# A two-layer token kernel on one Trainium2 core: token sums in PSUM columns, six chunks scaled by ScalarE, new engine orders in the paired part

## What is computed

```python
q     = relu(cond @ W3 + b3)                      # (64, 512), one row per batch
v_sum = sum(x, axis=1, keepdims=True)             # over the 64 tokens of a batch
x1    = (64 * x + v_sum) * q[:, None, :]          # the scaled input
y     = relu(x1 @ W2 + b2)                        # 4096 tokens, 512 x 512
out   = x + y @ W_base + b_base + (y @ A_s) @ B_s + sum_e gate_e * (y @ A_r[e]) @ B_r[e]
```

## Time and profile before

| what | us |
|---|---|
| median of 3 runs (240.29 to 241.37) | 240.49 |
| the profiled execution | 240.08 |
| its span, first to last instruction | 238.3 |
| TensorE busy | 227.8 (96%) |
| VectorE busy | 181.5 (76%) |
| GpSimd busy | 120.5 (51%) |
| ScalarE busy | 94.3 (40%) |
| mean granted TensorE clock | 0.986 |

### The profile page before, as it was taken

How to read it: one execution, slowest core, us unless ns; L and a number is a source line. 1 busy time by engine, 2 the same in 40 slices (tenths; PEclk the granted TensorE clock), 3 DMA queues, 4 the chain that set the end, 5 groups by cost and what they waited for, 6 DMA issues and landing times.

```text
span 238.3 us, 2849 instructions
## 1 busy us (share of the span) xinstructions
PE 227.8 (96%) x982; PEld 183.8 (77%) x982; DVE 181.5 (76%) x321; ACT 94.3 (40%) x181; POOL 120.5 (51%) x107
## 2 busy tenths in 40 slices
PE   7999999999999999999949999999899899999994
PEld 3877888888888888888836888888587678888883
DVE  0695799899799996999945699999995578482344
ACT  2369612736244512754135068243313465530010
POOL 4189323365219778699789203369988920000000
PEclk9999999999999999999995999999999999999999
DMA  6999905322294791044179135002155234002044
GB/s 204 323 226 228 255 13 130 70 89 91 35 216 179 231 263 25 1 174 178 26 170 194 44 133 178 0 0 33 21 191 176 88 105 164 0 7 47 11 179 176
DMA packets 32917, 29.05 MB, mean 122 GB/s; under 512 B 5841, under 2 KB 23317, under 8 KB 32902
## 3 DMA queue, kind: packets, MB, share of 16 engines
q1 hardware_dynamic: 31090, 28.69, 42.7%
q10 hardware_dynamic: 1812, 0.17, 0.6%
HBM read 18.89 MB, written 8.39 MB: 114 GB/s over the span
## 4 chain that ended last, share of the span: by engine, by line
PE 66%; POOL 15%; DVE 11%; ACT 3%; issue 2%; DVEq 0%; POOLq 0%; ACTq 0%
PE m_ps L1207 50%; PE hT L1207 7%; PE m_ps L1239 5%; POOL x_lo L483 4%; POOL xs L406 4%; DVE xs L942 3%; POOL x_lo_more L483 3%; DVE xs L928 2%; DVE x_nat L908 2%; POOL xs L496 2%; PE m_ps L1184 2%; POOL xs L502 2%; DVE vsum_pair L935 1%; POOL xs L489 1%; ACT y_hi L565 1%
## 5 line engine op out<-in xcount | busy, mean ns | idle before, releaser
L406 POOL TENSOR_TENSOR xs<-xs,qT 128x512 f32<-128x512 f32 x28 | 30.9, 1102 | 50.1 <-DVE xs L782 31.4
L1207 PE MATMUL m_ps<-Wb_lo,y_hi 128*128 128x512 f32 x116 | 45.1, 389 | 0.0
L1207 PE MATMUL m_ps<-Wb_hi,y_hi 128*128 128x512 f32 x116 | 45.1, 389 | 0.0
L1207 PE MATMUL m_ps<-Wb_hi,y_lo 128*128 128x512 f32 x116 | 45.1, 389 | 0.0
L565 ACT ACTIVATE y_hi<-m_ps,condT 128x512 fp32r<-128x512 f32 x30 | 20.8, 692 | 24.5 <-PE m_ps L1207 15.5
L1207 PEld LDWEIGHTS m_ps<-Wb_hi,y_lo 128*128 128x128 f32 x116 | 21.8, 188 | 4.6
L1207 PEld LDWEIGHTS m_ps<-Wb_lo,y_hi 128*128 128x128 f32 x116 | 21.8, 188 | 4.5
L1207 PEld LDWEIGHTS m_ps<-Wb_hi,y_hi 128*128 128x128 f32 x116 | 21.8, 188 | 4.5
L908 DVE TENSOR_TENSOR x_nat<-m_ps,x_nat 128x512 f32<-128x512 f32 x29 | 18.9, 682 | 7.3 <-PE m_ps L1207 7.3
L797 DVE TENSOR_TENSOR y_lo<-m_ps,y_hi 128x512 fp32r<-128x512 f32 x30 | 20.1, 675 | 5.4 <-ACT m_ps L566 5.4
L1207 PE MATMUL m_ps<-x_hi,W_hi 128*128 128x512 f32 x61 | 23.7, 389 | 0.0
(11 more groups left out here) (179 smaller groups left out, 486.0 us busy)
## 6 DMA issues: line engine op xcount, KB each, us to landing
out_dram<-x_nat SPq DMA_DIRECT2D x32, 256.0 KB, 2.1
x_quart<-in_x_dram SPq DMA_DIRECT2D x28, 256.0 KB, 5.0
x_nat<-in_x_dram SPq DMA_DIRECT2D x7, 1024.0 KB, 5.1
gatesT<-wT SPq DMA_DIRECT2D x24, 48.0 KB
x_nat<-in_x_dram SPq DMA_DIRECT2D x4, 256.0 KB, 3.8
W_f<-in_L_cond_W_dram SPq DMA_DIRECT2D x4, 256.0 KB, 6.6
Wb_f<-in_L_ffn_W_base_dram SPq DMA_DIRECT2D x1, 1024.0 KB, 9.3
W_sb<-in_L_cond_W_dram SPq DMA_DIRECT2D x2, 256.0 KB, 4.8
```

Source lines behind the costliest of these rows:

```text
L406: return nc.gpsimd.tensor_tensor(per_batch(tile), per_batch(tile), qT[:, c, BG * g:BG * (g + 1)].unsqueeze(2).to_broadcast([P, BG, N]), AL ...
L1207: mm = nc.tensor.matmul(psum, lhsT, rhs, start=start and i == 0, stop=stop and i == len(terms) - 1)
```

## The change

Names are those of the changed file; p is the pair, i the place in `CHUNKS`.

1. **Sums in PSUM.** `sums_of(p, i)` puts the eight token sums of a chunk in spare columns of a PSUM bank: all eight chunks in pair 0, chunks 1, 2 and 3 in pair 1 (the others stay in `vsum_pair`). The same for the last two chunks of group 3 (`sums_of_x`). TensorE waits before it writes such a bank until the sums are read (`wait_sums_read`, and a wait on `x1_sum_ready`).
2. **Six chunks scaled by ScalarE.** For the three chunks of each pair in `BY_SCALAR` VectorE no longer writes 64 x + sum over 128x512, but only `offset` = sum x q, 128x8; ScalarE then makes (64 q) x + offset in place, batch by batch, eight instructions of 128x64 (`make_chunk`). GpSimd does not touch these chunks. `q64` = 64 q is made once by ScalarE near the start.
3. **Orders.** VectorE handles chunk 3 of pair 0 before `y_rest_single(3, 0)`, and all chunks but chunk 7 ahead of `rank_experts(3)`; in the pairs `rank_experts`/`gates` go ahead of the sums of a chunk, `weigh(g)` behind chunk 4's transpose, `C11(0)` ahead of `weigh(3)`, and `total_next(0)` as a whole ahead of `add_x(3, 0, 1)`. ScalarE and GpSimd follow. TensorE's products keep their order; pair 1's first products wait for fewer `add_x`.

```diff
+        q64 = sb("q64", [P, KC, BG * (NG - PAIRED)])
+        offset = sb("offset", [P, 6, BG])
+        BY_SCALAR = (((0, 0), (1, 2), (0, 1)), ((0, 0), (0, 1), (1, 1)))
...
+        def sums_of(p, i):
+            cols = slice(400 + BG * i, 400 + BG * (i + 1))
+            if p == 0:
+                return m1_ps[1 if i in (4, 5) else 2][:, cols]
+            if i in (1, 2, 3):
+                return m1_pair[0][1][3][:, cols]
+            return vsum_pair[i % 2][:, :]
...
+            def make_chunk(p, half, c):
+                n = nth_by_scalar(p, half, c)
+                act.wait_ge(offset_ready, n)
+                for b in range(BG):
+                    toks = slice(b * N, (b + 1) * N)
+                    which = BG * (2 * p + half) + b
+                    nc.scalar.activation(xs[half][:, c, toks], xs[half][:, c, toks], ACT.Identity,
+                                         bias=offset[:, n - 1, b:b + 1],
+                                         scale=q64[:, c, which:which + 1]).then_inc(act_full_ready, 1)
...
             x1_split(3, 3)
+            make_chunk(0, 0, 0)
             operand(0, "x11", 0)
+            make_chunk(0, 1, 2)
+            operand(0, "T1", 0)
             relu(3, 0)
-            operand(0, "T1", 0)
...
                 operand_next("T4", 0)
                 operand_next("x11", 1)
+                if more:
+                    make_chunk(p + 1, 1, 1)
                 operand_next("x21", 1)
+                if more:
+                    hw_split(g + 1)
                 operand_next("T1", 1)
...
             def add_pair(p, i):
+                if by_scalar(p, i):
+                    g = PAIRED + 2 * p + half
+                    nc.vector.tensor_tensor(offset[:, nth_by_scalar(p, half, c) - 1, :], sums_of(p, i),
+                                            qT[:, c, BG * g:BG * (g + 1)], ALU.mult).then_inc(offset_ready, 1)
...
                 if p == 0:
+                    C11(0)
                     weigh(g - 1)
-                    C11(0)
                     u_2(0)
                     hw_rest(g - 1)
                     turn_next(0)
                     y_rest_pair(0, 0)
-                    sum_next(0)
+                    total_next(0)
                     add_x(g - 1, 0, 1)
...
                 if p > 0:
-                    pe.wait_ge(out_ready, TT * (g - 2) + TT)
+                    pe.wait_ge(out_ready, TT * (g - 2) + 2)
                 blocks(0, 1)
+                if p > 0:
+                    pe.wait_ge(out_ready, TT * (g - 2) + 3)
+                else:
+                    wait_sums_read(pe, 0, 4, 5)
                 blocks(0, 2)
```

More of the change, by code:

```diff
@@ L645, in operand @@
                 else:
-                    act.wait_ge(pair_full_ready, nth_chunk(p, {"x11": 0, "x21": 0, "x22": 1}[name], kk + (0 if name == "x11" else 2)))
+                    wait_full(act, p, {"x11": 0, "x21": 0, "x22": 1}[name], kk + (0 if name == "x11" else 2))
                 if p > 0:
@@ L690, in _ @@
             operand(0, "x22", 0)
+            operand(0, "T2", 0)
             relu(3, 2)
-            operand(0, "T2", 0)
             operand(0, "T3", 0)
+            operand(0, "x21", 0)
+            make_chunk(0, 0, 1)
             relu(3, 3)
-            operand(0, "x21", 0)
-            head(3)
             operand(0, "T4", 0)
             operand(0, "x11", 1)
+            head(3)
+            operand(0, "x21", 1)
             exponentials(3)
-            operand(0, "x21", 1)
             operand(0, "T1", 1)
@@ L1152, in pair @@
                 turn_next(2)
+                rank_experts(g)
+                gates(g)
                 total_next(2)
-                rank_experts(g)
                 turn_next(3)
-                gates(g)
                 total_next(3)
                 rank_experts(g + 1)
+                gates(g + 1)
                 turn_next(4)
-                gates(g + 1)
-                total_next(4)
+                weigh(g)
+                sum_next(4)
+                hw_rest(g)
+                add_next(4)
                 turn_next(5)
-                weigh(g)
-                sum_next(5)
-                hw_rest(g)
-                add_next(5)
+                total_next(5)
                 turn_next(6)
                 total_next(6)
-                add_x(g, 0, 1, 2, 3)
+                add_x(g, 0, 1)
                 turn_next(7)
+                total_next(7)
                 weigh(g + 1)
-                total_next(7)
-                hw_rest(g + 1)
+                if more:
+                    hw_rest(g + 1)
+                    add_x(g, 2, 3)
+                else:
+                    add_x(g, 2, 3)
+                    hw_rest(g + 1)
             for p in range(PAIRS):
@@ L1217, in m1 @@
                     pe.wait_ge(wT_ready, g)
+                    if g == PAIRED - 1:
+                        wait_sums_read(pe, 0, 0, 1, 2, 3)
+                elif m == 0 and g == PAIRED - 1:
+                    pe.wait_ge(x1_sum_ready, KC * (g + 1))
                 for k in range(KC):
@@ L1445, in pair @@
                 pe.wait_ge(wT_ready, g + 2)
+                if not last:
+                    wait_sums_read(pe, p + 1, 1, 2, 3)
                 m2(g + 1, 1, *range(KC))
```

116 lines of the change are left out of this document (79 added, 37 removed).

## The result

| | before | after |
|---|---|---|
| median of the runs | 240.44 (4 runs) | 233.83 (4 runs, 233.62 to 234.24) |
| ratio | | 0.972, 95% interval 0.969 to 0.975 |
| the profiled execution / its span | 240.08 / 238.3 | 233.62 / 231.9 |
| mean granted clock | 0.986 | 1.0 |
| TensorE busy | 227.8 | 225.0 (97%) |

A second measurement of the changed kernel, beside the kernel before at 241.22, gave 233.81 (ratio 0.970, 0.968 to 0.972). The prediction was 234.0, with a range of 230.6 to 236.6.

What follows compares the result with a forecast made beforehand. TensorE, busy 227.8 of 238.3, bounds the kernel; only 10.2 of idle or slowed time could be won. 240.08 - 5.2 (pair 0) - 1.3 (pair 1) = 233.6, with the median 0.4 above: 234.0, range 230.6 to 236.6.

Steps and rivals of the forecast that it cites:

- Sums in PSUM: VectorE's token sums with the addend in PSUM: 0.68 each against a mean of 1.13, saving VectorE 0.45 each.
- Pair 0, size: Pair 0 on TensorE: of 6.6 lost, 0.4 stays for T2's rest and 1.0 for u4, gain 5.2.
- The slow stretch: Pair 0, 127 to 131: ten matmuls at granted clock 0.50 after TensorE stood still 3.08; none expected behind 122.
- Pair 0, cause: Pair 0: its waits end with chunk 7, ready on VectorE at 120.6, then GpSimd's scale, T2 and rest.
- The step by step count: Pair 0 through VectorE, ScalarE and GpSimd: chunk 7 at 116.4 instead of 120.6, T2 at 119.2, its rest at 122.5.
- Pair 1, size: Pair 1 on TensorE: of 3.6 lost, 1.3 gained, with bounds 3.6 to -0.4.
- the sign named: Pair 1 on TensorE's timeline: T2's rest still waited for by 1 to 2.
- Offsets with both inputs in SBUF: Pair 1, VectorE's offsets of chunks 4 and 6: each delayed 0.6 by GpSimd, between bounds 0 and 1.25.
- the 235.3: Pair 1: the total time forecast if GpSimd holds both SBUF offsets in full.
- Pieces: ScalarE's 128x64 instructions: 0.45 long and 0.33 apart, so 2.75 a chunk (1.7 to 3.2).
- Rival D: Group 3 and pair 1: ScalarE's 128x64 instructions take 0.7, a chunk 5.7, so slower, 244.7; chance 0.05.
- Rival C: PSUM columns don't spare VectorE the hold, sums stay at 1.13, pair 0's slow clock stays: 237.8; chance 0.14.

Runs made afterwards that it cites:

- both parts undone: The changed kernel with token sums back in SBUF and all chunks scaled by GpSimd, only the new orders kept: 238.25.
- three moves: The changed kernel with chunk 0 turned behind u_4(0), add_x ahead of weigh(5), and x21's high part and chunk 5's scale earlier in pair 1: 233.97 together.

## Why the prediction came out right, and where its reasons did not

- **Pair 0, size.** Gain 5.2 foreseen, 5.3 measured. T2's rest 0.4 foreseen, 0.35 measured; u4 1.0 foreseen, 0.92 measured, behind the DMA and at the place named. T2 was ready within 0.1 of its time, and ScalarE's `copy_p1(0)` held its high part, as said. The slow stretch went.
- **Pair 0, cause: wrong in part.** The prediction said that chunk 7, ready at 120.6, ends these waits. VectorE's order alone brings it 2.7 earlier and T2 not at all. GpSimd's own list, through T2(0) and T1's rest to the last scale, reached chunk 7 at 122.03 in the kernel before, 1.4 after VectorE had it. The step by step count came out because it followed all three new lists, and that is not luck; the sentence on what bounds the stretch, had it been used to pick one edit, would have led to a kernel 1.6% slower.
- **Pair 1, size.** Gain 1.3 foreseen, 1.1 measured.
- **Pair 1, waits: the sum right, the sign of it wrong.** add_x(4, 2) was foreseen to hold product 2 by about 1 inside the loss for T2's rest: 1.27 measured. But the sign named was T2's rest waited for by 1 to 2, and 0.25 was left of it. Put in the old profile's times (5.5 added to the new ones there) x21's rest came at 177.0 (176.5 foreseen) and T2's rest ended at 185.6 (185.3). The two waits do hide each other, as the runs that moved add_x show, and the wait for hw_lo(5) hides with them.
- **Sums in PSUM.** 0.68 foreseen, 0.69 measured. Of the two left in SBUF in pair 1, foreseen over 1, chunk 5's took 1.24 and chunk 7's 0.69, with GpSimd idle for most of it. The sums in PSUM are worth 2.0 by the medians in the changed kernel; on the kernel before 0.9 by the profiled executions and 2.1 by the medians, and nothing in pair 0, where they were to count most.
- **Offsets with both inputs in SBUF.** A hold of 0.6 each was taken between 0 and 1.25. In pair 1 the two beside GpSimd took 1.07 and 1.15, about 0.9 and 1.0 of hold, near the upper end: 1.9 of hold where 1.2 was taken and 2.5 is the bound. The Trainium skill ("SBUF — State Buffer", Who interferes with whom) makes no exception for a short instruction, and the trace agrees, with 0.17 for the same instruction beside an idle GpSimd. The time did not go to the 235.3 that was worked out with it: x21's rest and T2's came only 0.5 and 0.3 later than foreseen, and most of the wait was hidden by add_x(4, 2). GpSimd's idle 2.42 ahead of x21's rest was no cushion, since it waits for that very chain: offset, pieces, x21's high part.
- **Pieces.** 0.45 long and 0.33 apart foreseen, 0.43 and 0.33 measured, 2.77 a chunk against 2.75. The Trainium skill ("VectorE: DVE Perf Modes", The TRN2 errata) has a fixed read latency exposed between instructions; here 0.10 of each 0.43 was overlapped, with source and destination in SBUF. With nothing overlapped the estimate would be a chunk of 8 x 0.432 = 3.5. That small pieces are dear the trace does bear out: eight take 2.77, while an ACTIVATE of 128x512 from SBUF takes 0.63. Rival D, pieces at 0.6 or more, is out.
- **The clock.** Rival C, that sums held as before keep the slow stretch, is out too: with sums in SBUF and even with both parts undone the clock held. The new orders are enough to keep TensorE from standing still for 3. That they are needed is shown only against the sums in PSUM: ScalarE's chunks in the old orders, alone or with those sums, were not run.

What stays open: which of the moves inside the three orders are needed. They were tried as whole lists only, VectorE's on one side and the other two on the other.

## What to carry to other kernels

When several engines work from fixed lists, the last wait on the timeline names the engine that came last, not the only one that would have been late. Before one list is changed, find out when each of the others would have reached the work, here GpSimd at 122.03 for a chunk ready at 120.6. New orders for engines that hand work to each other are one edit: half of it may be worse than none. And price the second and third wait in a stretch before moving the first; here three moves worth 2.9 on paper gave nothing that could be measured. When gains get small, compare profiles from a mark behind the first loads: two profiles of the same kernel agreed to 0.01 from there on and differed by 0.4 before it.

## What the runs showed of the hardware

- An instruction of eight columns can be held for most of a GpSimd instruction of 1.25: it took 1.07 and 1.15 with both inputs in SBUF beside a busy GpSimd, 0.17 with both in SBUF beside an idle one, and 0.17 with one in PSUM.
- A sum of 128x512 on VectorE with both inputs in SBUF took from 0.69 (GpSimd idle for most of it) to 1.77 (GpSimd busy throughout), in the same place of the list. Work taken off GpSimd is paid back in VectorE's time as well.
- TensorE stood 2.37 at one stretch and stayed at 1.00, and fell to 0.50 after 3.07, after 3.12, and after 2.41 that was followed by 1.07. In the kernel with ScalarE's and GpSimd's orders alone it fell after 2.15 (granted clock 0.69 in 112 to 116), having stood 0.54 shortly before, and again after 1.81 that was followed by 1.07 (0.50 in 132 to 136). One stop's length does not decide alone.
- The same load of x_quart held VectorE for 1.73, 1.81, 1.81, 2.03 and 2.46 in five profiles whose lists are the same up to there. A wait that ends with a transfer had this much spread, and it is as large as the last gains looked for here.
- The same loads at the start let VectorE begin between 7.06 and 7.91, and the whole execution shifts with it.
